# The maxima of a pair of heads are turned behind the next pair's products, and the side pieces are spread over the steps

## The reference, cut to what matters

```python
def xattn(x, z, Wq, Wk, Wv, Wo):          # L1_xattn (with biases) and L3_xattn (without)
    q = heads(x @ Wq)                     # 8 x 112 queries, 16 heads of 16
    k, v = heads(z @ Wk), heads(z @ Wv)   # 8 x 375 keys and values
    attn = softmax(einsum('bqhd,bkhd->bhqk', q, k) * 0.25, axis=-1)
    return merge(einsum('bhqk,bkhd->bqhd', attn, v)) @ Wo
x = x + xattn(layernorm(x), ctx, ...)
```

## Time and profile before

| | |
|---|---|
| median of 3 runs | 2354.99 us (2353.04 to 2358.04) |
| profiled execution, own time | 2357.41 us |
| its span | 2355.4 us |
| TensorE busy (matmul) | 2037.8 us, 87% |
| VectorE, ScalarE, GpSimd busy | 1332.3, 840.4, 715.1 us |
| first stage | 737.2 to 944.4 us of the span |
| second stage | 2034.3 to 2241.5 us of the span |
| mean granted TensorE clock | 0.862 |

### The profile page before, as it was taken

The page is one execution under the profiler, slowest core; times in us unless marked ns, Lnnn a source line. Parts: engine busy times, 40 slices in busy tenths (PEclk is TensorE's granted clock), DMA queues, the critical chain, the costliest instruction groups (busy, mean ns, idle before and its releaser), DMA issues.

```text
span 2355.4 us, 59884 instructions
## 1 busy us (share of the span) xinstructions
PE 2037.8 (87%) x24096; PEld 1488.1 (63%) x24096; DVE 1332.3 (57%) x3559; ACT 840.4 (36%) x3000; POOL 715.1 (30%) x1608
## 2 busy tenths in 40 slices
PE   8999998989987877898978798998999998787744
PEld 4899998867565655467866655665645555465523
DVE  6667676755265675545645615784370403567587
ACT  2455554533173333212334514664111112133322
POOL 3566664221011444101345503330000002345511
PEclk9555556999997999799998988998999999699956
DMA  3000001003000000300020000000200000000000
GB/s 134 4 5 5 5 5 77 2 21 158 4 2 8 8 12 2 134 1 23 1 110 22 2 1 8 11 8 2 113 35 1 0 0 4 7 8 12 2 0 16
DMA packets 8033, 57.35 MB, mean 24 GB/s; under 512 B 792, under 2 KB 5248, under 8 KB 5984
## 3 DMA queue, kind: packets, MB, share of 16 engines
q1 hardware_dynamic: 7760, 53.54, 5.9%
HBM read 52.62 MB, written 0.92 MB: 23 GB/s over the span
## 4 chain that ended last, share of the span: by engine, by line
PE 68%; DVE 17%; issue 6%; ACT 5%; POOL 3%; DMA 1%; POOLq 0%; DVEq 0%; SPq 0%; ACTq 0%
PE banks L274 42%; PE banks L1395 9%; PE banks L279 5%; PE banks L2028 3%; DVE memory L2128 3%; PE banks L1548 1%; PE banks L2035 1%; DVE memory L2146 1%; DVE memory L1278 1%; DVE memory L3054 1%; DVE memory L1497 1%; ACT memory L2118 1%; ACT memory L2109 1%; PE banks L968 1%; PE banks L1699 1%
## 5 line engine op out<-in xcount | busy, mean ns | idle before, releaser
L274 PE MATMUL banks<-memory 128*112 128x256 f32 (+9 forms) x4192 | 1147.0, 427 | 143.6 <-ACT memory L2109 39.3
L274 PEld LDWEIGHTS banks<-memory 128*128 128x128 f32 (+4 forms) x4192 | 698.7, 194 | 502.2 <-issue 340.7
L1395 PE MATMUL banks<-memory 128*128 128x8 bf16 (+2 forms) x10752 | 313.2, 175 | 7.8 <-DVE memory L1480 1.4
L279 PE MATMUL banks<-memory 112*112 112x112 f32 (+3 forms) x1328 | 219.3, 283 | 112.1 <-DVE memory L855 27.7
L1395 PEld LDWEIGHTS banks<-memory 128*128 128x128 bf16 x10752 | 300.1, 104 | 21.5 <-POOL memory L1454 11.7
L279 PEld LDWEIGHTS banks<-memory 112*112 112x112 f32 (+3 forms) x1328 | 156.9, 157 | 205.6 <-issue 64.9
L2118 ACT ACTIVATE memory<-banks 125x672 f32<-125x672 f32 x128 | 93.5, 731 | 238.2 <-PE banks L2035 238.2
L1497 DVE TENSOR_REDUCE memory<-banks 128x48 f32<-128x192 f32 x448 | 122.0, 291 | 61.9 <-PE banks L1395 41.3
L2128 DVE TENSOR_REDUCE memory<-banks 112x2 f32<-112x750 f32 x128 | 120.4, 941 | 44.4 <-PE banks L2028 42.5
L2196 POOL TENSOR_TENSOR memory<-memory 125x224 f32<-125x224 f32 x128 | 84.1, 657 | 180.6 <-ACT memory L2118 179.5
L2028 PE MATMUL banks<-memory 32*112 32x375 f32 x512 | 123.0, 554 | 3.4 <-DVE memory L2143 1.6
(11 more groups left out here) (266 smaller groups left out, 2909.7 us busy)
## 6 DMA issues: line engine op xcount, KB each, us to landing
memory<-in_l2x SPq DMA_DIRECT2D x1, 7680.0 KB, 21.2
memory<-in_l2f SPq DMA_DIRECT2D x1, 7168.0 KB, 20.2
memory<-in_l1f SPq DMA_DIRECT2D x1, 4617.0 KB, 14.8
memory<-in_ctxT SPq DMA_DIRECT2D x24, 187.5 KB
memory<-in_l2f SPq DMA_DIRECT2D x1, 4096.0 KB, 12.8
memory<-in_l3f SPq DMA_DIRECT2D x1, 3073.0 KB, 22.1
memory<-in_l2a SPq DMA_DIRECT2D x1, 3072.0 KB, 19.5
memory<-in_l0f SPq DMA_DIRECT2D x1, 2304.0 KB, 9.1
```

The costliest lines, as they stand in the source:

```text
L274: ins = self.nc.tensor.matmul(out, weights[i], acts[i], start=i == 0, stop=i == n - 1)
L279: return self.nc.tensor.transpose(out, in_, self.ident[0:n, 0:n])
L1395: ins = self.nc.tensor.matmul(own[:, part:3, at:at + B], self.whh[:, part, l, j, g * P:(g + 1) * P], self.upper[l][:, 0:3 - part, j * B:(j ...
```

## The change

In `order()` the turn and add of pair n+1 stand behind cross n, and the max of pair n+2, which is a step "top" of its own, behind them. On VectorE the order add n+1, max n+2 stays as it was; on TensorE the turn of n+1 moves from ahead of cross n to behind it. The side pieces are spread so that no step has two that use bank 7. In the prologue "stats" goes ahead of "parity". `CrossL3` yields its "row" (VectorE's statistics and GpSimd's normalization of a finished row) behind the cross of step 5 of a batch, so it now comes ahead of the add and the max of that step. Two branches that did nothing are gone, and the steps that they named fall through to a parent that does nothing for them either.

```diff
-    prologue = (("parity", 0), ("stats", 0), ("xn", 0), ("kk", 0), ("xT", 0), ("q", 0))
+    prologue = (("stats", 0), ("parity", 0), ("xn", 0), ("kk", 0), ("xT", 0), ("q", 0))
-    plan = ((("xT", 0, 1), ("stats", 0, 2)), (), (("q", 0, 1),), (("kk", 0, 1), ("xn", 0, 2), ("y", 0, -1)), (), (),
-            (("vv", 0, 1),), (("kk", 1, 1), ("v", 2, 1)))
+    plan = ((("xT", 0, 1), ("stats", 0, 2)), (), (("q", 0, 1),), (("kk", 0, 1), ("xn", 0, 2)), (("y", 0, -1),),
+            (("vv", 0, 1),), (("kk", 1, 1),), (("v", 2, 1),))
...
             b, i = divmod(n, 8)
+            yield "cross", b, n
             if n + 1 < self.pairs:
                 yield "peak", (n + 1) // 8, n + 1
-            yield "cross", b, n
+            yield "top", b, n + 2
             if n >= 4 and n % 4 < 2:
...
-        elif step == "cross":
-            if i + 2 < self.pairs:
-                self.dve_peaks(i + 2)
+        elif step == "top":
+            if i < self.pairs:
+                self.dve_peaks(i)
...
-        elif step == "kk":
-            pass
-        elif step == "weighted":
-            pass
```

## The result

The changed kernel takes **2322.56 us** (median, 2316.51 to 2324.40) against 2354.33 of the kernel before in the same session: a ratio of 0.9858, 95% interval 0.9836 to 0.9881. It is faster, and inside the range, but 13 us above the forecast of 2309.5. Of the 45.8 us promised, the profiled executions show 32.9 (spans 2355.4 and 2322.5). Source lines moved with the edit: score is L2029 now, turned score L2036, the reader of keys L2110, exp L2119, max L2129, add L2144, reciprocal L2147.

A forecast was written before the change was run, and what follows sets the result against it. Waits, with no engine full, were taken to bound the kernel; a batch falls from 22.83 to 19.65 us. Two stages at 22.9 gain 45.8: 2357.4 - 45.8 = 2311.6, with the median 2.4 lower 2309.5 us, range 2300 to 2326.

The forecast's parts named there:

- Both waits of 1.40: In each batch, before v and before y, TensorE idles 1.40 us for ScalarE reading bank 7; both go.
- The "row" of the second stage: VectorE's row statistics ahead of an add: moves about 0.85 us, costs nothing; uncovered it would cost 5 us.
- the move: Turn of the next pair behind cross: a bare step costs 1.93 us in place of 2.21, 1.3 us per batch.
- Rival 2: Turn, add and cross hand over slower than said, every step keeps about 2.2 us: 2328 us; chance 0.17.
- the forecast's own case: All terms as forecast, unknown handovers saving about 3 us or costing 8: 2306 to 2318 us; chance 0.68.
- free openings: Rival at the stage openings: xn starts 3.5 us earlier, 7 us for both stages, 2302.5 us; chance 0.09.
- rival 3: TensorE's clock falls to 1.2 GHz within a stage, a batch costs about 29 us; chance 0.04 slower, 0.02 same.
- step 3: Batch step with the keys: add 9.05 to 9.33, next cross at 9.47 us; keys on TensorE, to 9.40, covered.
- step 2: Batch step with the queries: add waits for the norm, next cross at 7.37 us; max to 8.21, q to 9.02.
- Steps 2, 6 and 7: Batch steps with queries, keys and v: the middle one 1.93 or 1.98 us, the last releasing the next batch at 19.65.
- the prologue: Stage opening with stats first: xn starts near 742 if held as before; gain taken as zero.
- pair 63: End of a stage: the last cross waits for its add, up to 0.8 us, mostly beside GpSimd's sums; 0.1 lost.

The follow-up runs named there:

- plan_only: The kernel before with the new plan of side pieces, nothing else: 2334.58 us, ratio 0.9905.
- order_only: The changed kernel with the plan and the prologue of before: 2365.95 us, ratio 1.0038.
- old_prologue: The changed kernel with parity ahead of stats again, as before the change: 2322.51 us, ratio 0.9856.
- swap_q_kk: The changed kernel with the keys a step earlier and the queries a step later, exchanged: 2310.84 us, ratio 0.9805.
- filler_small_after: The changed kernel with 3 more matmuls, read by nobody, ahead of the keys: 2311.55 us, ratio 0.9816.
- swap_hold: The changed kernel with queries and keys exchanged and GpSimd's memsets held behind the first xn: 2300.53 us, ratio 0.9768.
- filler_small_order: The changed kernel with the old plan and prologue, plus 3 extra matmuls ahead of the keys and 6 ahead of y: 2371.24 us, ratio 1.0070.

## Why the prediction was right, and where it wasn't

**Right: the two mechanisms.** Both waits of 1.40 went, with 0.28 left ahead of v (forecast: less than 0.6). The max releases nobody. Exp starts the next products; from 815.67 to 817.51 the step is 1.84 where I had 1.93, since exp (816.73 to 817.46) hands over in 0.05 and not in 0.14. The add behind the norm makes one idle of 0.82 (forecast: about 1). With undisturbed clock a batch is 19.81 against 19.65. The "row" of the second stage cost nothing: its batch is 19.81 too. plan_only and order_only say that the shares are 2.17 and 0.85, not 1.9 and 1.3, and that the move pays only once the plan has taken the long waits out. Rival 2 (the move worth nothing, 2328) is refuted: old_prologue and plan_only differ in the move alone, and their ratios are 0.9856 [0.9842, 0.9870] and 0.9905 [0.9893, 0.9917].

**Luck: the range.** 2322.56 lies outside the 2306 to 2318 that I gave the forecast's own case. It is inside 2300 to 2326 because I had widened that range for free openings and for rival 2, and neither came true. What filled the room was the clock, for which the range had no part.

**Wrong: rival 3 at a chance of 0.06.** The failed term is the clock, taken at its upper level in batches 1 to 7 of both stages; six of these fourteen batches hold a stretch at the lower level, 9.0 us in all. I argued from the longest idle, which shrank from 1.40 to 1, and from TensorE's busy share, which rose. The rows of batches 1 to 6 show that neither decides. Before, a batch had the two idles of 1.40 and between them these two, each some 3 us from the next, and all twelve ran at 1.00:

```profile
830.92 0.32 PE L279 MATMUL banks<-memory 112*128 112x112 f32 x1 [0.64 <-DVE memory L2128]
...
834.09 0.32 PE L279 MATMUL banks<-memory 112*128 112x112 f32 x1 [0.94 <-DVE memory L2128]
```

After it, with idles of 0.82 and 0.62 that are 1.8 us apart, four in twelve did not. I had also looked at one batch in the middle of each stage only; batch 7 of the kernel before would have shown that the clock can fall inside a stage. The size was wrong too: I had priced a fall as a whole batch at the lower level (9 to 10 us), and each cost 1.5. The Trainium skill (TensorE: Matmul & The Clock Gate, on psum-queue depth-cycling) says that frequent short idles between groups of matmuls made the clock of one kernel oscillate between its two levels, and that falling back and warming up again between the groups cost it throughput. I had set it aside since the rows of before showed 1.00; the rows of after and of order_only, with 4 and 12 falls in batches 1 to 6, agree with it.

What is shown for the changed kernel: take the second idle away, by another order (swap_q_kk) or by work that computes nothing (filler_small_after), and the slow stretches of batches 1 to 6 go from four to none. filler_small_after speaks against the rival that the swap won by its shorter steps, as its steps are the old ones. What stays open: which series of idles brings a fall and which doesn't. The same steps give a fall in batches 1, 3 and 5 and none in 2, 4 and 6; the wait of 1.40 ahead of v brought none before and five in order_only; and batch 7 of swap_hold, with the same steps in both stages, holds a slow stretch in the second and none in the first. No fillers were tried ahead of v.

**Wrong: step 3.** I let the keys start with TensorE's own work (2.10 for the step), at 8.50 on my clock. They wait 0.62 for the queries' reader in bank 7, which the max and the late norm have pushed back: measured 2.62 (806.95 to 809.57). My own step 2 had that reader end at 9.02; with 0.14 and 0.90 behind it the step comes to 2.69, so the wait could have been read off the working. Steps 2, 6 and 7 took 2.87, 1.84 and 2.04 in place of 3.10, 1.99 and 2.15, so most of that error cancels, by luck; over the batch it is 0.16, over twelve about 2.

**Wrong in small: the prologue.** Zero was taken, by the held instruction of the earlier trace rows, and the reading was right: xn at 742.54, within the range named. But the late masks hold the reader of the keys and so xT, which I had not followed: 1.8 lost in the two stages together. And pair 63 waits for its add and the max ahead of it longer than allowed, 1.53 from pair 62 in place of 0.7 to 0.9.

## What to carry to other kernels

Where one PSUM bank is shared by all side pieces, write down for each piece who reads the piece before it and what that reader is queued behind; moving pieces apart by steps isn't enough when the reader's own engine is late. When the idles of TensorE are cut up, look at where they then stand: here some tenths of a microsecond in two places close together brought a slow stretch of 1.5 us in 9 of 36 batches, and whether an idle matters can be tried with a few matmuls into free columns, if they are no longer than the idle. Where large memsets of GpSimd open a stage, try them behind the first short VectorE instructions that the chain needs: here that gave 5.9 us for two stages.

## What the runs showed of the hardware

- A stretch at the lower clock inside a stage (matmuls slow from 828.6 to 832.6 in the batch shown) costs 1.5 us a time (19.81 against 21.31) and begins behind an idle: at most 0.7 us behind one of 0.61 or 0.62 in the changed kernel, up to 1.9 us behind ones of 1.40 in order_only and filler_small_order. In batch 7 of the kernel before it stands behind one of 2.09.
- A VectorE tensor_scalar on 128 x 2 numbers takes 0.17 us alone and 3.68 when it starts 0.4 ahead of GpSimd's memsets: in the trace it starts before them and is held all the same. The maxima, beside GpSimd's sums or not, took 0.92 to 0.94 throughout.
- Three float32 matmuls of 64 columns on 128 x 128 weights take 0.79 us and six 1.45, while the two of 375 columns for the keys take 0.87: here a small filler was not cheap by the column, which made my first fillers twice too long.
- From ScalarE's exp to the TensorE matmul that waited for it 0.05 us passed, less than the 0.14 from its reader of the keys.
